# The second choice of routed experts, from its sigmoid on, two slots later

## What is computed

```python
s = sigmoid(router_in @ W_router.T)          # 8 values a token
_, topk_idx = top_k(s + router_bias, 2)
gates = s_sel / (denom + 1e-09)              # of the two chosen
shared: h = silu(x @ s_w1.T) * (x @ s_w3.T);  out += h @ s_w2.T      (2 experts)
routed: h = gelu(x @ r_w1.T);                 out += h @ r_w2.T * gate (8 experts)
out = (shared / 2 + routed) / 4
...
P = out @ U1;  H = gelu_tanh(P @ V1 + b1);  Q = H @ U2;  x + Q @ V2 + b2
```

## Time and profile before

| | us |
|---|---|
| median of 3 runs (lowest to highest) | 890.29 (889.94 to 890.36) |
| profiled execution, its time | 891.2 |
| its span | 889.4 |
| TensorE busy | 870.8 (98%) |
| VectorE busy | 683.9 (77%) |
| ScalarE busy | 573.5 (64%) |
| POOL busy | 401.0 (45%) |

### The profile page before, as it was taken

One profiled execution on the slowest core, in us unless ns is written; L12 is line 12 of the kernel. 1 busy time (PEld: TensorE's weight loads), 2 busy tenths in 40 slices (PEclk: granted clock), 3 DMA queues, 4 the chain that ended last, 5 costly groups with the idle time before them and its releaser, 6 DMA issues.

```text
span 889.4 us, 12606 instructions
## 1 busy us (share of the span) xinstructions
PE 870.8 (98%) x3838; PEld 689.8 (78%) x3838; DVE 683.9 (77%) x1096; ACT 573.5 (64%) x1029; POOL 401.0 (45%) x374
## 2 busy tenths in 40 slices
PE   8999999999999999999999999999999999999997
PEld 5777888777888888888888888888888777777773
DVE  7877777869689786686686686686666887998887
ACT  6888888765555455555555555555555678989795
POOL 7547783125356453253253252252232326754462
PEclk9999999999999999999999999999999999999999
DMA  9589981024113112012012012011010049571700
GB/s 306 205 280 305 296 292 45 1 85 134 49 48 111 38 46 83 1 47 83 1 48 83 1 48 83 0 48 48 1 48 0 1 111 197 113 179 52 161 25 36
DMA packets 36404, 83.23 MB, mean 94 GB/s; under 512 B 4464, under 2 KB 14320, under 8 KB 34544
## 3 DMA queue, kind: packets, MB, share of 16 engines
q1 hardware_dynamic: 36336, 82.42, 30.4%
HBM read 71.39 MB, written 6.83 MB: 88 GB/s over the span
## 4 chain that ended last, share of the span: by engine, by line
PE 77%; DVE 8%; issue 4%; SPq 4%; ACT 4%; DMA 2%; POOL 1%; DVEq 0%; ACTq 0%
PE ps L931 16%; PE ps L950 16%; PE ps L936 16%; PE ps L991 8%; PE ps L986 8%; PE ps L993 8%; DVE HL L1572 2%; SPq L657 2%; PE ps L973 1%; PE ps L971 1%; ACT HH L1083 1%; DMA TMP<-scratch 1%; SPq L770 1%; DVE Hf L1552 1%; DVE Hf L1559 1%
## 5 line engine op out<-in xcount | busy, mean ns | idle before, releaser
L1077 ACT ACTIVATE Sg<-ps 128x512 f32<-128x512 f32 x288 | 171.7, 597 | 242.7 <-PE ps L950 242.3
L1552 DVE TENSOR_TENSOR Hf<-ps,Sg 128x512 f32<-128x512 f32 x288 | 198.0, 688 | 146.2 <-ACT Sg L1077 95.4
L1657 POOL TENSOR_TENSOR HL<-Hf,HH 128x512 fp32r<-128x512 f32 x130 | 174.2, 1347 | 171.1 <-ACT HH L1083 154.2
L1083 ACT ACTIVATE HH<-Hf 128x512 fp32r<-128x512 f32 x346 | 216.2, 625 | 22.4 <-DVE Hf L1552 14.6
L1572 DVE TENSOR_TENSOR HL<-Hf,HH 128x512 fp32r<-128x512 f32 x248 | 220.7, 890 | 4.3 <-ACT HH L1083 3.2
L931 PE MATMUL ps<-XHL,WBH 128*128 128x512 f32 x512 | 203.9, 398 | 2.0 <-DVE Hf L1552 1.9
L950 PE MATMUL ps<-XHL,WBH 128*128 128x512 f32 x512 | 202.1, 395 | 0.0
L936 PE MATMUL ps<-XHL,WBL 128*128 128x512 f32 x512 | 202.0, 395 | 0.0
L1672 POOL TENSOR_TENSOR XT<-XT,TMP 128x512 f32<-128x512 f32 x64 | 84.3, 1317 | 250.8 <-DVE TMP L1426 250.7
L931 PEld LDWEIGHTS ps<-XHL,WBH 128*128 128x128 f32 x512 | 96.0, 188 | 27.6 <-DVE Hf L1552 4.3
L950 PEld LDWEIGHTS ps<-XHL,WBH 128*128 128x128 f32 x512 | 96.0, 188 | 23.0
(11 more groups left out here) (275 smaller groups left out, 1326.7 us busy)
## 6 DMA issues: line engine op xcount, KB each, us to landing
CWB<-scratch SPq DMA_DIRECT2D x14, 1024.0 KB, 4.7
GWD<-expert_down SPq DMA_DIRECT2D x21, 576.5 KB, 4.6
GWU<-expert_up SPq DMA_DIRECT2D x21, 514.0 KB, 5.4
CWB<-scratch SPq DMA_DIRECT2D x40, 256.0 KB, 6.1
ST<-in_wb_dram SPq DMA_DIRECT2D x8, 768.0 KB, 6.3
ST<-scratch SPq DMA_DIRECT2D x24, 256.0 KB, 8.8
GX<-XT SPq DMA_DIRECT2D x68, 64.0 KB, 2.9
XT<-in_x_dram SPq DMA_DIRECT2D x8, 256.0 KB, 5.2
```

The costliest lines, as they stand in the source:

```text
L1077: e.activation(Sg[:, it.n % NG, :], zb[z % NZ][:, :], ACT.Silu).then_inc(s_act, 1)
L1083: e.activation(HH[:, it.n % NH, 0:it.cols], hidden_place(it), ACT.Copy).then_inc(s_hi_act, 1)
L1552: e.tensor_tensor(Hf[:, it.n % NS, :], zb[z % NZ][:, :], Sg[:, it.n % NG, :], ALU.mult).then_inc(s_prod, 1)
L1657: e.tensor_tensor(HL[:, it.n % NH, :], Hf[:, it.n % NS, :], HH[:, it.n % NH, :].bitcast(F32), ALU.subtract).then_inc(s_lo_pool, 1)
```

## The change

The list of slots of the second choice starts at S2.2 instead of S2.0. All ten entries move by two slots: the sigmoid from the slot of S2.0 to that of S2.2, the VectorE steps from S2.1 to S3.3 to S2.3 to F0.1, the transpose from F0.1 to F0.3, and the copy with its DMA from F0.2 to F1.0.

```diff
         pick = [[lag_b[3] + 1 + i for i in (0, 1, 2, 3, 5, 6, 7, 8, 10, 11)],
-                [pos["S", 2, 0, 0].k + i for i in (0, 1, 2, 3, 4, 5, 6, 7, 9, 10)]]
+                [pos["S", 2, 1, 0].k + i for i in (0, 1, 2, 3, 4, 5, 6, 7, 9, 10)]]
```

## The result

The changed kernel takes 893.53 us (median of 6 runs, 891.79 to 895.24), the kernel before 890.02 (6 runs). The ratio is 1.0038, 95% interval 1.0028 to 1.0049: 3.4 us slower, where I had forecast 2.1 us slower, and 0.1 us outside my range of 890.2 to 893.4. The direction and the waits came as forecast; a term of the sum was missing.

What follows compares the result with a forecast made beforehand. TensorE, 77% of the chain, was taken as the bound, losing time only in stalls. The late copy's 3.1 us leaves 2.2, small waits take 0.1 off: +2.1 us on 890.29 gives 892.4, range 890.2 to 893.4.

Steps and rivals of the forecast that it cites:

- ScalarE's part: SiLUs of S2.0, S2.1: TensorE's 1.41 us stall goes; one more table load, +1.28 us, and a 0.9 us wait come.
- rival (c): Table switches around the sigmoid each drain as the skill page says: +4.8 us, 895.1 us; chance 0.02.
- The choice: VectorE's 23 small steps, L1346 to L1395, end at 764.0 against 761.83; TensorE's transpose waits 0.5 to 1.6 us.
- The clash I subtracted as possibly gone (L1389): VectorE's L1389 held by POOL's residual, about 1.0 us; if it falls away, the steps could end at 763.0.
- The copy: VectorE's L1398, behind two cast-subtraction pairs, ends at 769.1; F0.0's down product on TensorE waits, 3.1 us late.
- T: End of VectorE's copy of the turned gates (L1398), which releases TensorE at F0.0's down product; forecast 769.1.
- the mean price of a pair: VectorE's cast and subtraction beside POOL's residuals: 2.27 us, the mean of three, against 1.07 alone.
- (a): VectorE's copy comes in time, T 765.5 to 767.6: a wash, -0.3 to +0.7 us, 890.5 us; chance 0.25.
- the faster one (b): SiLU stall of 1.41 goes, no new 0.9 wait, copy in time: -1.4 us, 888.9 us; chance 0.05.
- How much of it stays: From F0.0's down product to the routed tiles: of TensorE's 3.1 us delay about 2.2 stay.
- so about 2.2 of the 3.1 us stay: First routed tiles: ScalarE, not TensorE, paces them, so its 2.2 us lateness remains of TensorE's 3.1.
- T + 2.8: Start of ScalarE's table load for the routed Gelu, 2.8 us behind the copy's end; 2.2 us later than before.

Runs made afterwards that it cites:

- The first experiment: Changed kernel with F0's first down product waiting for L1395, the last step using its PSUM bank, not for the copy: 891.54 us, ratio 1.0018.
- the fourth: Kernel before with only the VectorE steps, transpose and copy two slots later, sigmoid left in S2.0's slot: median 894.76 us, ratio 1.0048.
- the sixth: Changed kernel with the residuals of F0.1 and F0.3 on VectorE instead of POOL: 890.87 us, ratio 1.0013.
- fifth experiment: Changed kernel with nine useless matmuls put ahead of F0's first down product, where TensorE waits for the copy: ratio 1.0025.
- third: Changed kernel with the transpose and the copy one slot sooner, at F0.2 and F0.3: ratio 1.0019.
- seventh: Kernel before with the residuals of F0.1 and F0.3 on VectorE instead of POOL: ratio 1.0000.

## Why the prediction was right or wrong

**ScalarE's part was right.** The stall of 1.24 us behind the SiLU went, one of 0.89 came at S3.0 (I said 0.9), with one table load more. Each load around the sigmoid took 1.28 and the next instruction started 0.01 behind its end. The Trainium skill (ScalarE: Activation LUTs, What ACT_TABLE_LOAD costs) gives 2.66 us a switch; this trace doesn't show it, and rival (c) was rightly low.

**The choice: right.** L1395 was done at 765.37 - 1.03 = 764.34, I had 764.0. The clash I subtracted as possibly gone (L1389) went and came back two steps sooner on L1380, 1.18 us. The transpose waited 1.69, just over my 0.5 to 1.6.

**The copy: right.** I took its end, T, at 769.1, halfway from 768.8 by the mean price of a pair to 769.4, and the release of TensorE at 769.2; they are 769.94 + 0.28 - 1.03 = 769.19 and 769.24. The first experiment shows that this wait, with the fall of the clock behind it, is the larger part of the loss, the fourth that the loss comes without the third table load, the sixth that POOL makes the wait long. The rival that the copy comes in time (a) and the faster one (b) are out.

**How much of it stays: here the prediction failed.** The step was "so about 2.2 of the 3.1 us stay", resting on ScalarE, not TensorE, pacing the first routed tiles, with TensorE 2 us ahead of it. TensorE's clock was no term of my sum at all. It fell to 0.50: seven steps from one matmul to the next took 2.99 us (771.13 to 774.12) instead of 7 x 0.2325 = 1.63. ScalarE's load came at T + 3.1 instead of T + 2.8, as the matmuls of F1.2 and F1.3 that it needs were slow ones (0.49 and 0.63 us long). So it was 2.62 us late where I had 2.2, and behind it TensorE, which had used up what it had in hand, paced the tiles for 0.82 us more, where I had put nothing. With the clock kept up the region is 2.4 us longer (fifth experiment, and the fourth's profile), all of it ahead of the load, which is what my sum was for: I had 2.1. The fall of the clock is the 1.05 us beyond it, 60.45 - 59.40.

The clock does not explain the spread of the times. The changed kernel's run with a mean clock of 1.00, which had no such fall, took 893.88 us, the second longest of the six, and its fastest, 891.79, had 0.998. Executions differ ahead of the region: the first table load starts anywhere from 744.19 (third) to 747.71 (seventh) in the twelve profiles, with no edit ahead of it.

I had looked at the clock only as the page of before gave it, 0.999, and took over from it that stalls cost their own length. The longest stall there was 1.24 us; I forecast two of up to 1.6 and 3.1 us close together, and that should have been a case of its own.

**The split of the 3.44 us**, from the regions: 1.05 the clock (change less fifth), 1.18 the wait for the copy (fifth less first), 1.21 what the first experiment leaves, by its waits those for L1395 and for F0.2's residual less what was gained at the SiLU. These are differences of single profiles; by the ratios the three are about 1.2, 0.6 and 1.6 us, so no more is sure than that each is of the order of a microsecond.

## What to carry to other kernels

When an operation is moved later in a fixed order, follow each result it makes to every semaphore that guards something with it: here a buffer's next user waited for an event two steps behind the buffer's last use, harmless for as long as it was early. Name the last reader itself in such a wait. And give new stalls of TensorE as long as these a case of their own in which the clock falls behind them: in the profiles, filling the stall with idle matmuls gave back a microsecond by itself.

## What the runs showed of the hardware

Behind a stall of 2.40 us the clock came down in one profile (third experiment, 0.66 on the mean of 764 to 768), behind waits of 1.69 and 2.83 us in another (the change, 0.50 through 772 to 774), and behind 0.81 and 3.23 us it stayed at 1.00 in a third (the fourth experiment). So the length of the stall alone does not decide it here. The changed kernel itself goes either way, as one of its six runs had a mean clock of 1.00. A VectorE operation held by POOL ended a fixed time behind POOL's end: 0.03 us for a 128x16 scalar operation, 0.28 for a 128x512 cast, 0.54 for a 128x512 residual. That is less than the whole operation takes alone (0.17, 0.43, 0.69).
